# Layer 2's first edge pass: unread bf16 products on TensorE behind every chunk and during the fill, and four PSUM banks of sums instead of five

## What is computed

```python
def _gat_layer(x, src, dst, W, a_src, a_dst, concat):
    for h in range(W.shape[0]):
        Wh = x @ W[h]
        es, ed = Wh @ a_src[h], Wh @ a_dst[h]
        e = jax.nn.leaky_relu(es[src] + ed[dst], 0.2)
        att = _seg_softmax(e, dst, n)
        out = jax.ops.segment_sum(att[:, None] * Wh[src], dst, num_segments=n)
        outs.append(out)
    if concat:
        return jax.nn.elu(jnp.concatenate(outs, axis=-1))
    return jnp.mean(jnp.stack(outs, axis=0), axis=0)

def _rel_gcn_layer(x, src, dst, w, W):
    deg = jax.ops.segment_sum(w, dst, num_segments=n)
    norm = w / jnp.maximum(deg[dst], 1e-16)
    h = x @ W
    agg = jax.ops.segment_sum(norm[:, None] * h[src], dst, num_segments=n)
    return jax.nn.relu(agg)

for i in range(2):
    x1 = _gat_layer(x1, src, dst, ..., concat=i != 1)
    x2 = _rel_gcn_layer(x2, src, dst, edge_weight, gcn_params[i])
return jnp.maximum(x1, x2)
```

## Time and profile before

| | us |
|---|---|
| median of three runs without a profile | 2941.07 (2940.23 to 2944.43) |
| the profiled execution, first to last instruction | 3321.3 |
| first edge pass of layer 2 in it, first turn to last product | 897 to 1558 |
| second edge pass | 1601 to 2301 |
| diffusion | from about 2415 |

### The profile page before, as it was taken

How to read it: one execution, slowest core, us unless ns; L and a number is a source line. 1 busy time by engine, 2 the same in 40 slices (tenths; PEclk the granted TensorE clock), 3 DMA queues, 4 the chain that set the end, 5 groups by cost and what they waited for, 6 DMA issues and landing times.

```text
span 3321.3 us, 56445 instructions
## 1 busy us (share of the span) xinstructions
PE 2643.0 (80%) x15058; PEld 1980.1 (60%) x15146; DVE 1663.3 (50%) x6677; ACT 980.3 (30%) x4757; POOL 1410.3 (42%) x1667
## 2 busy tenths in 40 slices
PE   2444545598448888889499998989699999999998
PEld 1444444455337787778367776767566666666665
DVE  4555555597334555554244545444854444444442
ACT  2444555465212333333123333333800000000000
POOL 3666666300156666661445656660232222222210
PEclk9999999999655555555695667677899999999999
DMA  2111111163233333331423333332610000000001
GB/s 77 44 44 45 44 45 44 44 227 114 79 82 91 89 92 92 91 89 46 106 70 83 90 84 90 89 89 59 231 59 18 17 18 18 18 17 18 17 28 42
DMA packets 183897, 227.24 MB, mean 68 GB/s; under 512 B 62447, under 2 KB 146488, under 8 KB 182808
## 3 DMA queue, kind: packets, MB, share of 16 engines
q0 software_dynamic: 50176, 131.74, 14.8%
q1 hardware_dynamic: 122654, 86.45, 8.3%
q10 hardware_dynamic: 10746, 5.37, 0.6%
HBM read 183.92 MB, written 39.48 MB: 67 GB/s over the span
## 4 chain that ended last, share of the span: by engine, by line
PE 62%; DVE 10%; issue 9%; another core or an unknown queue 5%; ACT 3%; ACTq 2%; DMA 2%; SPq 0%; DVEq 0%; POOL 0%; POOLq 0%
PE banks L2510 26%; PE banks L1538 7%; PE banks L1599 4%; PE banks L1596 3%; PE banks L1597 3%; PE banks L1602 2%; PE banks L748 2%; PE banks L1600 2%; DMA arena<-dst_flat 2%; PE banks L537 1%; PE banks L540 1%; DVE arena L524 1%; PE banks L1554 1%; PE banks L2521 1%
## 5 line engine op out<-in xcount | busy, mean ns | idle before, releaser
L2510 PE MATMUL banks<-arena 128*128 128x384 bf16 (+1 forms) x5475 | 879.8, 324 | 0.0
L2510 PEld LDWEIGHTS banks<-arena 128*128 128x128 bf16 x5475 | 535.7, 98 | 341.7
L222 POOL DMA_INDIRECT arena<-value_table,arena x392 | 396.4, 1011 | 487.2 <-DMA ed_table<-arena 267.0
L222 POOL DMA_INDIRECT arena<-gat_table,arena x392 | 389.7, 994 | 347.1 <-PE banks L1602 169.0
L222 POOL DMA_INDIRECT arena<-h_table,arena x392 | 371.8, 948 | 218.0 <-PE banks L540 90.9
L537 PE MATMUL banks<-arena 128*128 128x425 bf16 x392 | 201.8, 515 | 310.2 <-DVE arena L524 179.6
L2493 POOL TENSOR_TENSOR arena<-arena 128x128 f32<-128x128 f32 x225 | 103.3, 459 | 647.5 <-DVE arena L2567 638.2
L2561 DVE TENSOR_REDUCE arena<-banks 128x128 f32<-128x384 f32 x225 | 125.3, 557 | 364.3 <-PE banks L2510 356.7
L1538 PE MATMUL banks<-arena 128*128 128x512 bf16 (+1 forms) x902 | 279.3, 406 | 17.6 <-issue 15.3
L2551 ACT ACTIVATE arena<-arena 128x128 bf16<-128x128 f32 (+1 forms) x200 | 61.9, 309 | 732.4 <-DVE arena L2567 732.4
L1596 PE MATMUL banks<-arena 128*128 128x17 f32 x784 | 227.6, 371 | 43.3 <-issue 27.2
(11 more groups left out here) (282 smaller groups left out, 4601.6 us busy)
## 6 DMA issues: line engine op xcount, KB each, us to landing
adj_rows<-arena SPq DMA_DIRECT2D x1, 20000.0 KB, 54.6
arena<-adj_rows SPq DMA_DIRECT2D x2, 7200.0 KB, 22.0
arena<-h_rows SPq DMA_DIRECT2D x225, 64.0 KB, 1.8
arena<-ed_table SPq DMA_DIRECT2D x784, 0.5 KB
arena<-h_table,arena POOLq DMA_INDIRECT x392
arena<-value_table,arena POOLq DMA_INDIRECT x392
arena<-gat_table,arena POOLq DMA_INDIRECT x392
arena<-adj_rows SPq DMA_DIRECT2D x2, 1600.0 KB, 6.2
```

The costliest lines, as they stand in the source:

```text
L222: return e.indirect_dma_start(into, None, table, bass.IndirectOffsetOnAxis(ap=index.bitcast(U32), axis=0))
L2510: x = e.matmul(acc[:, 0:w], C[:, sb, db * P:(db + 1) * P], old[:, sb, 0:w], start=(sb == 0), stop=(sb == LAST))
```

## The change

`busy` loses its condition and issues its products in both passes. Bank 7, into which they go, is no longer one of the banks of sums, so the first pass goes round the four banks of the second. The whole diff:

```diff
@@ -1340,8 +1340,8 @@
             NGR = -(-NC // PER)
             last_of = lambda g: min(PER * g + PER, NC) - 1
 
-            NBK = 4 if i else 5
-            bank_of = lambda c: (4, 5, 6, 1, 7)[c // PER % NBK]
+            NBK = 4
+            bank_of = lambda c: (4, 5, 6, 1)[c // PER % NBK]
@@ -1533,9 +1533,8 @@
 
                 def busy(*columns):
 
-                    if i:
-                        for n in columns:
-                            e.matmul(banks[:, 7, 0:n], identb, spare[:, 0:n], start=True, stop=True, skip_group_check=True)
+                    for n in columns:
+                        e.matmul(banks[:, 7, 0:n], identb, spare[:, 0:n], start=True, stop=True, skip_group_check=True)
 
                 busy(*[512] * 24)
```

## The result

| | us |
|---|---|
| changed kernel, median of 4 runs | 3151.47 (3149.02 to 3154.18) |
| kernel before, median of 4 runs | 2942.75 (2940.23 to 2953.20) |
| ratio | 1.0693 (95%: 1.0661 to 1.0724) |
| profiled execution of the changed kernel | span 3149.2, run 3151.05 |

The change makes the kernel 209 us, 6.9%, slower; 156 were forecast, and 3097 us, in a range of 2955 to 3180. The span of the profiled execution of the changed kernel is 2 us from its median, while that of the kernel before was 380 us above its own. The two can't be compared side by side, and the experiments had to find a profile of before that can. They ran on three chips: the kernel before took 3292 us on chip 3, 3319 on chip 7 and 2951 on chip 4. Which chip the comparison above and the first profile of before ran on isn't recorded.

The account below looks back on a forecast made before the run. The first edge pass was taken as bound by TensorE at the lower clock, then by gathered rows. Steady part +139, first batches -12, tail +25, fill +4 gave +156 us: 3097 us, range 2955 to 3180.

Parts of the forecast that it names:

- The sign and the main mechanism: First edge pass: clock stays at the lower level for nearly the whole pass, TensorE pays for the pairs; slower, chance 0.80.
- rival B: First edge pass: higher clock holds throughout, gathers bind at 10.0 us a batch; -110 us, 2831 us; chance 0.16.
- The batch after: First pass's steady part with the pair: 15.7 us a batch at the lower clock, bounds 14.5 and 16.2.
- The batch before: First pass's steady part without the pair: 12.46 us a batch, of which TensorE idles 2.0; floor 10.5.
- I carry the difference over unchanged: Whole kernel: +156 us against the profiled 3321.3 us span is added to the median, 2941 + 156 = 3097.
- The first batches at the higher level, -12: First pass, first two or three batches after the fill: higher clock, 10.0 to 12 us each, saving 12 us.
- Why it falls: First pass after its fill: clock drops once TensorE starves, within two or three batches, when gathered stock is used up.
- The tail: End of the first pass: forty chunks left, TensorE alone the bound, 0.62 us a chunk, +25 us.
- The fill: Start of the first pass: added 512-column products mostly lie beside waits; +4 us, bounds 0 to +12.
- Four banks: First pass's sums in four banks instead of five: about three chunks of slack remain before stores; 0 us.
- A: Rival: first pass's clock changes back and forth as in the second pass; +38 us, 2979 us; chance 0.11.
- C: Rival: first pass's added products fall only into idle time, needing 5.0 us a batch against 2.0; chance 0.03.

Follow-up runs that it names:

- the pair alone: Changed kernel without the fill's unread products in the first edge pass, pair behind every chunk kept: 3429.06 us, ratio 1.0395 to the kernel before on chip 3.
- the second profile: Profile of the changed kernel run again unaltered, beside the kernel before on chip 4: 3157.20 us, ratio 1.0696.
- the fill's products alone: Changed kernel without the pair behind each chunk in the first edge pass, products of the fill kept: 3303.81 us, ratio 1.0036 to the kernel before on chip 3.

## Why the prediction came out as it did

- **The sign and the main mechanism: right.** The clock stands at 0.50 through the whole steady part, TensorE becomes the bound without a gap, the gathers wait for it. The other way round would have been rival B, 2831 us. The Trainium skill (TensorE: Matmul & The Clock Gate, Why this matters for your kernels) says that a TensorE kept busy without a break gets its full clock. The runs disagree with that: the kernel with the pair alone was busy 600.00 of 600.00 us at 0.50.
- **The size: too small, and it came as close as it did partly by luck.** 156 us were forecast and 209 measured. Two errors stand in the steady part, of opposite sign: the batch before was taken 1.93 us too long, which hides 83 us of the loss, and the batch after 0.85 us too long, which takes 37 of them back. The rest are the smaller terms below.
- **The batch after: too long.** 15.7 forecast, 14.85 measured; with the rows' own times the chunk is 1.55 and not 1.71. I had counted 0.12 a chunk at most for a weight load hidden behind the pair, and 0.16 were hidden (0.45 to 0.29 for the first f32 product). Eight chunks at 1.55 are 12.4, so the other work came to 2.5 where I took 1.8: where that work stands between pair and sums the load isn't hidden, and the pair itself takes 0.75 instead of 0.62 (1099.51 to 1100.26 in the same view). The lower bound of 14.5 held; "batches of 15 to 16 us", named as the sign of being right, was just missed.
- **The batch before: too long as well, and this is the step that failed.** "I carry the difference over unchanged": the 12.46 us are those of an execution of 3321 us, and 12.34 and 12.53 were measured on the two chips on which before takes 3292 and 3319. Where it takes 2951, the batch is 10.53, TensorE's own 10.5 of the earlier trace rows. I had named this case (up to +84 us) and left it out of the forecast. With both corrected the steady part is 43 x (14.85 - 10.53) = +186 and not +139. The profiled span itself, 380 us above the median, should have been reason enough to take the floor; with the 15.7 left as it was, that would have made some 3180 us, 30 above what was measured.
- **The first batches at the higher level, -12:** the two behind batch 4's turn take 14.96 and 12.39 us, the ones behind them 14.91, so 2.5 us came back, which the mean of 14.85 holds already. The fill's products still stand in the first of them, and the level fell soon behind the last of those.
- **Why it falls: wrong.** I said that the level holds "only while TensorE never starves", and that it would starve within two or three batches. It fell between 852.3 and 852.4 us with TensorE running. In order of time, from the last three products of the fill (847.51) to the first pair at the lower level:

```profile
847.51 0.81 PE L1537 MATMUL banks<-arena 128*128 128x512 bf16 x3
848.16 0.29 PE L1595 MATMUL banks<-arena 128*128 128x17 f32 x2
...
851.72 0.27 PE L1537 MATMUL banks<-arena 128*128 128x256 bf16 x1 [0.16 <-issue]
851.83 0.29 PE L1595 MATMUL banks<-arena 128*128 128x17 f32 x2
851.97 0.38 PE L1596 MATMUL banks<-arena 128*128 128x17 f32 x2
852.27 0.19 PE L1601 MATMUL banks<-arena 128*27 128x17 bf16 x1
852.40 0.82 PE L1537 MATMUL banks<-arena 128*128 128x512 bf16 x2
853.01 0.45 PE L1595 MATMUL banks<-arena 128*128 128x17 f32 x2
```

  The row of a pair is 0.50 us long in the fill and 0.82 from 852.40 on. The one gap, of 0.16, is no gap: a pair stands there, and the record of its first product is missing. In the second profile TensorE is busy 32.00 of 32.00 us up to 852 and goes on without idling, and there too the level falls, at about 853.4. So faster gathers would not have saved rival B; its point of decision was put in the wrong place. What changed ahead of the fall is that the fill's products of 512 columns ended. Between the sums, one pair of products left the level at 0.50, two of 512 did so too, and three of 512 brought a mean of 0.69; what exactly the chip goes by is not shown.
- **The tail:** +25 forecast, +20.3 measured, 0.51 a chunk instead of 0.62, by the hidden weight load again (1.55 - 1.09 = 0.46, and the other work).
- **The fill:** +4 forecast; +7.1 - 4.4 = +2.7 measured on the quick chip, and +12 (4 to 20) for the fill's products alone on a slow one, at the end of my bounds.
- **Four banks:** 0 forecast, and no difference that can be told measured.
- **Rivals.** A (back and forth) didn't come with the pair; it came with three products of 512, at +196 us on a slow chip. B and C didn't come.

## What to carry to other kernels

Before products are added to keep TensorE's clock up, count twice what a batch costs: at the lower level with them, and at the higher level with them, and compare the second with the batch as it is. Here it was 14.85 against 10.53, and with the three products of 512 that move the clock a batch takes 11.27 even at the higher level; there was nothing to win. And where a profiled execution is far from the median of the runs, take the engine's own floor from its rows as the likeliest batch, and not the mean with its waits.

## What the runs showed of the hardware

- Busy isn't enough for the clock, and a fall needs no gap. TensorE at 600.00 of 600.00 us with chunks of f32 products of 17 columns and a pair of 512 and 256 stayed at 0.50; with three products of 512 in place of the pair it was at the higher level for 38% of the time. It fell from 1.00 to 0.50 at the end of the fill with TensorE busy on both sides of the fall.
- The same kernel takes 12% longer on some chips: 2951 us on one (and 2942 on one that isn't recorded), 3292 and 3319 on two others. The batch of the first pass is 12.3 to 12.5 us there instead of 10.5. Where the time goes is in part visible, why it goes there is not. In SyncE's queue (start, us from the first to the last of a line's DMAs) the eight window loads of 32-byte rows are drawn out beside the gathers: 6.3 to 6.8 us on the mean in the profiles with 12.3 to 12.5 us a batch, 4.1 in that of the kernel without unread products on chip 4. But with the pair, on the same slow chip 3, they take 4.0. The longest in the steady part of the first profile of before, one on chip 4 and one with the pair on chip 3:

```profile
1247.18 9.30 SPq L1378 DMA_DIRECT2D arena<-ed_table  x8
```

```profile
959.39 3.83 SPq L1378 DMA_DIRECT2D arena<-ed_table  x8
```

```profile
1219.65 3.83 SPq L1378 DMA_DIRECT2D arena<-ed_table  x8
```

  That these loads cause the difference is not shown, and they can't cause all of it: the first turn of the windows, ahead of which none of them stands, comes at 882 to 897 us on the slow chips and at 784 to 785 on chip 4 in the kernels that have no products ahead of it. Two rows for a stretch of the first layer's edge pass (layer 0), in which SyncE issues nothing, in the first profile of before and in that of the changed kernel (the code of this pass is the same in both):

```profile
200.00:400.00 200.00, 100.72 (x402) 83.84 (x401) 104.79 (x532) 99.93 (x398) 126.06 (x133) 1.00 0.17 45
```

```profile
200.00:400.00 200.00, 146.19 (x480) 93.03 (x479) 131.35 (x639) 120.07 (x479) 151.24 (x161) 1.00 0.21 53
```

  At the same clock 133 gathers are done in 200 us instead of 161, while a gather's own instruction takes as long on both (945 and 944 ns, median). So the slower passes are those that gather at the full pace, with window loads beside them or without; with the pair the batch is 14.91 us on chip 3 and on chip 4 alike.
- On chip 4 the second pass's own unread products take its clock to a mean of 0.86 to 0.88 and its batch to 10.4 to 10.7 us (three profiles), and without any the batch is 10.7 at 0.50: the higher clock is spent on the products that raise it.
